# Edge lists laid out as 384 consecutive edges a partition, and tile 0 prepared ahead of a branch, in a graph attention and mixture-of-experts kernel

## The reference, cut to what matters

```python
def _gat_layer(x, W, a_src, a_dst, b, src, dst, n_nodes):
    h = x @ W
    e = leaky_relu((h @ a_src)[src] + (h @ a_dst)[dst], 0.2)
    m = segment_max(e, dst); w = exp(e - m[dst]); z = segment_sum(w, dst)
    return segment_sum(h[src] * (w / z[dst])[:, None], dst) + b
```

## Time and profile before

| what | us |
|---|---|
| median of 3 runs | 1493.97 (1488.02 to 1497.21) |
| the profiled execution | 1489.21 |
| its span | 1487.5 |
| PE busy | 1375.7 (92%) |
| DVE busy | 1126.6 (76%) |
| ACT busy | 914.1 (61%) |
| POOL busy | 436.6 (29%) |
| granted clock, mean | 0.975 |

### The profile page before, as it was taken

One profiled execution on the slowest core, in us unless ns is written; L12 is line 12 of the kernel. 1 busy time (PEld: TensorE's weight loads), 2 busy tenths in 40 slices (PEclk: granted clock), 3 DMA queues, 4 the chain that ended last, 5 costly groups with the idle time before them and its releaser, 6 DMA issues.

```text
span 1487.5 us, 25322 instructions
## 1 busy us (share of the span) xinstructions
PE 1375.7 (92%) x8889; PEld 1319.7 (89%) x8889; DVE 1126.6 (76%) x1543; ACT 914.1 (61%) x1601; POOL 436.6 (29%) x335
## 2 busy tenths in 40 slices
PE   2996999899799999899999999999998997799997
PEld 2995988899699999799999999999997997699997
DVE  5888998635889653586868868778688887788885
ACT  6887777322467322447847568486687421699995
POOL 1000000000000010335636446265476400355553
PEclk9997999999899999999999999999999998799999
DMA  7001000221334620000000000000011596376651
GB/s 202 8 1 42 16 25 23 71 92 38 105 94 145 195 86 0 22 1 2 21 1 21 0 0 21 0 21 0 0 32 40 154 294 146 118 169 166 162 103 26
DMA packets 48640, 99.17 MB, mean 67 GB/s; under 512 B 7178, under 2 KB 23182, under 8 KB 48554
## 3 DMA queue, kind: packets, MB, share of 16 engines
q1 hardware_dynamic: 40787, 75.04, 16.2%
q0 software_dynamic: 7488, 22.26, 7.5%
q10 hardware_dynamic: 279, 0.77, 0.2%
HBM read 67.23 MB, written 33.70 MB: 68 GB/s over the span
## 4 chain that ended last, share of the span: by engine, by line
PE 65%; DVE 6%; issue 3%; ACT 2%; DMA 2%; POOL 1%; ACTq 0%; POOLq 0%; SPq 0%; DVEq 0%
PE ps L421 13%; PE ps L422 13%; PE ps L423 13%; PE ps L912 5%; PE ps L957 4%; PE ps L959 4%; PE ps L958 3%; PE ps L936 3%; PE ps L938 3%; DVE mcol L1181 1%; POOL prlo L1144 1%; PE ps L1370 1%; PE ps L661 1%; DVE prlo L1144 1%; ACT prob L1082 1%
## 5 line engine op out<-in xcount | busy, mean ns | idle before, releaser
L1144 POOL TENSOR_TENSOR prlo<-prob,prhi 125x500 fp32r<-125x500 f32 x180 | 257.0, 1434 | 250.1 <-ACT prob L1082 249.2
L1181 DVE TENSOR_REDUCE mcol<-ps 125x1 f32<-125x1250 f32 x120 | 175.0, 1459 | 76.2 <-PE ps L912 74.1
L1080 ACT ACTIVATE prhi<-ps 125x500 fp32r<-125x500 f32 x300 | 176.8, 589 | 72.0 <-PE ps L938 65.3
L957 PE MATMUL ps<-prhi,vhi 125*128 125x250 f32 x600 | 171.6, 286 | 10.4 <-POOL prlo L1144 6.9
L1082 ACT ACTIVATE prob<-ps 125x500 f32<-125x500 f32 x300 | 176.1, 587 | 0.7 <-DVE prlo L1144 0.6
L959 PE MATMUL ps<-prlo,vhi 125*128 125x250 f32 x600 | 168.0, 280 | 0.0
L958 PE MATMUL ps<-prhi,vlo 125*64 125x250 f32 x600 | 167.0, 278 | 0.0
L936 PE MATMUL ps<-qst,kst 128*125 128x250 f32 x600 | 155.7, 283 | 2.7 <-ACT val L614 1.1
L421 PE MATMUL ps<-hhi,pthi 125*125 125x384 f32 x400 | 155.0, 388 | 3.0 <-DVE ptlo L784 3.0
L938 PE MATMUL ps<-q,k 128*125 128x250 f32 x600 | 153.4, 280 | 0.0
L1666 POOL MEMSET q<- 128x2500 f32 x1 | 2.2, 2185 | 503.3 <-PE ps L423 503.3
(11 more groups left out here) (343 smaller groups left out, 3849.7 us busy)
## 6 DMA issues: line engine op xcount, KB each, us to landing
w1all<-in_L_ffn_W_dram SPq DMA_DIRECT2D x8, 1152.0 KB, 9.0
w2st<-in_L_ffn_W_dram SPq DMA_DIRECT2D x8, 1152.0 KB
wqst<-in_L_ffn_Wqkv_dram SPq DMA_DIRECT2D x12, 384.0 KB, 4.2
hid_d<-tin SPq DMA_DIRECT2D x10, 375.0 KB
hin<-hid_d SPq DMA_DIRECT2D x10, 375.0 KB
vtin<-xn_d SPq DMA_DIRECT2D x10, 375.0 KB
out_dram<-accr POOLq DMA_DIRECT2D x10, 375.0 KB, 8.3
xres<-in_x_dram SPq DMA_DIRECT2D x10, 336.0 KB
```

The lines of the kernel that those rows point to most:

```text
L957: pe.matmul(ps[:, b:b + GQ], vhi[:, e, kt, :], hi, start=kt == 0, stop=False)
L1080: act.activation(prhi[:, n % RING, :], bank(3 + n % 3, P, 2 * GQ), ACT.Exp, scale=float(HD) ** -0.5)
L1144: eng.tensor_tensor(prlo[:, n % RING, :], prob[:, n % 3, :], prhi[:, n % RING, :].bitcast(f32), ALU.subtract)\
L1181: dve.tensor_reduce(mcol[:, e, t:t + 1], ps[0:P, 0:N], AX.X, ALU.max, negate=True).then_inc(sem("max"), 1)
```

## The change

1. **Edge layout.** One partition holds 384 consecutive edges: `sraw` is [128, 384], `draw` [128, 62 + 384]. Loads: destinations rows 1 to 95 (1784 bytes each), sources rows 0 to 95 (1536 bytes), the first destination row; then, after GpSimd (POOL) has set rows 96 to 127, rows 96 to 106 of both, and the last partial row of both: seven loads for eight. The transposes are still six of 128 x 128, now into banks 4 and 5, and the copy out of them writes with a stride of three columns.
2. **Copies over two engines.** ACT copies and divides the sources (`edges_src`), DVE copies the destinations alone.
3. **Tile 0 ahead of the branch.** Its moments go from ACT to DVE (MOMENTS_DVE starts at 0), its scale, normed copy, transposes, upper and lower half stand ahead of the branch, as does the first `ohs` batch. PE turns tile 0 before it waits for the flag.
4. **Order of ACT before the loop.** Only 8 edge values are made before it (20 before); in the loop two a step until it is 20 ahead (`digits_until`). All six `whi` and normed tile 1 stand before the loop.
5. **Products of tile 0.** `first1` takes all products with `whi` first (24, chunk by chunk), then the 12 with `wlo`.
6. **Places.** FIRST 8 to 0, with it all projections, the handover and the first turn eight steps earlier (TURN0 151 to 143); TURN 31 to 32; `destinations(b)` at least 5b + 1 for 4b - 3; WEIGHT1_AT, moments and scales moved as below.

```diff
-FIRST, PERIOD, PARTS = 8, 12, 13
-TURN0, TURN, EARLY, SLOTS = FIRST + 143, 31, 12, 21
+FIRST, PERIOD, PARTS = 0, 12, 13
+TURN0, TURN, EARLY, SLOTS = FIRST + 143, 32, 12, 21
-MOMENTS_DVE = tuple(range(2, T, 2))
+MOMENTS_DVE = tuple(range(0, T, 2))
-WEIGHT1_AT = (2, 3, 5, 6, 7, 9)
+WEIGHT1_AT = (5, 6, 9, 10, 11, 13)
+def digits_until(g):
+    return min(g + min(AHEAD, 8 + g), STEPS)
...
+            sp.dma_start(draw[1:96, :], dst_rows(1, 96)).then_inc(sem("edges_in"), 16)
+            sp.dma_start(sraw[0:96, :], src_rows(0, 96)).then_inc(sem("edges_in"), 16)
+            sp.dma_start(draw[0:1, MOST:], dst[0:384].rearrange("(p k) -> p k", p=1)).then_inc(sem("edges_in"), 16)
             sp.wait_ge(sem("set_pool"), ERAW_CLEAR)
+            sp.dma_start(draw[96:full, :], dst_rows(96, full)).then_inc(sem("edges_in"), 16)
+            sp.dma_start(sraw[96:full, :], src_rows(96, full)).then_inc(sem("edges_in"), 16)
+            sp.dma_start(draw[full:full + 1, 0:MOST + some], dst_rows(full, full + 1, MOST + some)).then_inc(sem("edges_in"), 16)
+            sp.dma_start(sraw[full:full + 1, 0:some], src[384 * full:EDGES].rearrange("(p k) -> p k", p=1)).then_inc(sem("edges_in"), 16)
...
+            def first1(i):
+                for n in range(3 * i, 3 * i + 3):
+                    if n < 4 * KD:
+                        k, h, x1 = n // 4, n // 2 % 2, (txhi, txlo)[n % 2]
+                        if n % 4 == 0:
+                            pe.wait_ge(sem("w_hi"), k + 1)
+                        pe.matmul(bank(4 + h, P, HALF), x1[:, 0, k * P:(k + 1) * P], whi[:, k, h * HALF:(h + 1) * HALF],
+                                  start=n < 4 and n % 2 == 0, stop=False)
+                    else:
+                        k, h = n // 2 - 2 * KD, n % 2
+                        if h == 0:
+                            pe.wait_ge(sem("w_lo"), k + 1)
+                        last = pe.matmul(bank(4 + h, P, HALF), txhi[:, 0, k * P:(k + 1) * P], wlo[:, k, h * HALF:(h + 1) * HALF],
+                                         start=False, stop=k == KD - 1)
...
-                        if t and g == linear(t - 1, 0):
+                        if t and g == linear(t - 1, 6 if t == 1 else 0):
                             transposes1(t)
...
+            moments1(1)
+            act.wait_ge(sem("start_pe"), EDGES_T)
+            act.activation(edge[:, 0, LEAD:].rearrange("q (p c) -> q c p", c=3), bank(4, 128, 384).rearrange("q (c p) -> q c p", c=3), ACT.Copy)\
+                .then_inc(sem("edges_src"), 1)
+            act.wait_ge(sem("edges_src"), 1)
+            act.activation(digit[:, 0, :], edge[:, 0, 0:NCOLS], ACT.Identity, scale=1.0 / DIGITS, bias=viol[:, 6:7])\
+                .then_inc(sem("edges_src"), 1)
+            root1(0)
+            rooted1(1)
+            normed(0)
+            weights1(0)
+            higher1(0)
             act.wait_ge(sem("start_dve"), VALUES)
             for g in range(4):
                 valued(g)
+            weights1(1)
+            weights1(2)
+            valued(4)
+            valued(5)
+            weights1(3)
+            valued(6)
+            valued(7)
+            weights1(4)
+            weights1(5)
+            normed(1)
...
-                if g + AHEAD < STEPS:
-                    valued(g + AHEAD)
+                for q in range(digits_until(g), digits_until(g + 1)):
+                    valued(q)
-                    if t >= 2 and g == max(linear(t - 3, 6), 4 * t + 3):
+                    if t >= 2 and g == max(linear(t - 3, 6), 4 * t):
-                    if t and g == linear(t - 1, 4):
+                    if t and g == linear(t - 1, 9 if t == 1 else 4):
                         higher1(t)
-                    if t and g == linear(t - 2, 9):
+                    if t >= 2 and g == max(linear(t - 2, 9), 10):
                         normed(t)
...
+            dve.wait_ge(sem("edges_in"), 112)
+            dve.tensor_copy(efl[:, 1, :, :], draw[:, MOST:].rearrange("p (c k) -> p c k", c=3))
+            dve.tensor_copy(efl[:, 0, :, :], sraw[:, :].rearrange("p (c k) -> p c k", c=3)).then_inc(sem("start_dve"), 1)
...
+            moments1(0)
+            dve.wait_ge(sem("start_pe"), EDGES_T)
+            order.did(dve.tensor_copy(edge[:, 1, LEAD:].rearrange("q (p c) -> q c p", c=3),
+                                      bank(5, 128, 384).rearrange("q (c p) -> q c p", c=3)))
...
+            rstd1(0)
+            dve.wait_ge(sem("rows_paired"), 2)
+            destinations(0)
+            dve.wait_ge(sem("edges_src"), 2)
...
+            step_near(0)
+            lower1(0)
+            spread = dve.value_load(flag[0:1, 0:1], min_val=0, max_val=1)
```

More of the change, by code:

```diff
@@ L183, in build @@
     mcol = put("mcol", [P, 2, T], f32)
-    viol = put("viol", [128, 6], f32)
+    viol = put("viol", [128, 8], f32)
     FREE = top[0]
@@ L243, in build @@
     assert put.end <= FREE + 2 * 4 * KD * N + 32
-    sraw = put("sraw", [128, 3, 128], i32, at=FREE)
-    draw = put("draw", [128, 3, MOST + 128], i32, at=put.end)
+    sraw = put("sraw", [128, 384], i32, at=FREE)
+    draw = put("draw", [128, MOST + 384], i32, at=put.end)
     efl = put("efl", [128, 2, 3, 128], f32, at=put.end)
@@ L1425, in _ @@
         def _(sp):
[L1427 to L1434, removed]
@@ L1764, in _ @@
                 for c in range(3):
-                    last = pe.transpose(ps[:, a * BANK + c * 128:a * BANK + (c + 1) * 128], efl[:, a, c, :], ident[:, :])
+                    last = pe.transpose(ps[:, (4 + a) * BANK + c * 128:(4 + a) * BANK + (c + 1) * 128], efl[:, a, c, :], ident[:, :])
             last.then_inc(sem("start_pe"), 1)
[L1767 to L1772, removed]
             def transposes1(t):
@@ L1787, in triple1 @@
                 if t == 0:
-                    pe.wait_ge(sem("w_lo"), k + 1)
+                    first1(i)
+                    return
                 last = three(pe, bank(4 + 2 * u + h, P, HALF), txhi[:, u, k * P:(k + 1) * P], txlo[:, u, k * P:(k + 1) * P],
@@ L1859, in first_layer @@
                                 triple_sum(pe, 0, t, t % 2, i)
+            transposes1(0)
+            pe.wait_ge(sem("start_dve"), VIOL)
+            for c in (0, 4, 5):
+                last = pe.matmul(ps[0:1, 2 * BANK:2 * BANK + 1], viol[:, c:c + 1], viol[:, 1:2], start=c == 0, stop=c == 5)
+            last.then_inc(sem("start_pe"), 1)
+            pe.wait_ge(sem("start_dve"), FLAG)
+            spread = pe.value_load(flag[0:1, 0:1], min_val=0, max_val=1)
             pe.wait_ge(sem("set_pool"), TABLES)
@@ L2151, in _ @@
             order.did(dve.memset(viol[:, 2:3], FAR))
+            order.did(dve.memset(viol[:, 6:7], 0.5 / DIGITS - 0.5))
             dve.wait_ge(sem("set_pool"), ERAW_CLEAR)
[L2153 to L2161 removed]
             def relative(j):
@@ L2382, in first_layer @@
                         lower2(dve, 0)
-                    if near and g < STEPS:
+                    if near and 0 < g < STEPS:
                         step_near(g)
+            s_, d_ = edge[:, 0, 0:NCOLS], edge[:, 1, :]
+            quarter, node, value = (digit[:, i, :] for i in range(3))
+            real = slice(LEAD, LEAD + EROWS)
+            dve.wait_ge(sem("edges_in"), 112)
+            dve.tensor_copy(efl[:, 1, :, :], draw[:, MOST:].rearrange("p (c k) -> p c k", c=3))
+            dve.tensor_copy(efl[:, 0, :, :], sraw[:, :].rearrange("p (c k) -> p c k", c=3)).then_inc(sem("start_dve"), 1)
@@ new lines, in _ @@
+            order.wait()
+            order.did(dve.scalar_tensor_tensor(lohi[:, 0, real], d_[:, real], 0.0, lohi[:, 0, real], ALU.add, ALU.is_lt,
+                                               accum_out=viol[:, 0:1]))
+            order.did(dve.scalar_tensor_tensor(lohi[:, 1, real], d_[:, real], 0.0, lohi[:, 1, real], ALU.add, ALU.is_ge,
+                                               accum_out=viol[:, 4:5]))
+            relative(0)
+            order.wait()
+            dve.sem_inc(sem("start_dve"), 1)
@@ new lines, in _ @@
+            rstd1(0)
+            dve.wait_ge(sem("rows_paired"), 2)
+            destinations(0)
+            dve.wait_ge(sem("edges_src"), 2)
+            order.did(dve.tensor_scalar(node, quarter, ROUNDER, -ROUNDER, ALU.add, ALU.add))
+            order.wait()
+            order.did(dve.scalar_tensor_tensor(value, node, -float(DIGITS), s_, ALU.mult, ALU.add))
+            order.did(dve.tensor_copy(scol[:, :], node))
+            order.wait()
+            dve.wait_ge(sem("start_pe"), VIOL_SUM)
@@ new lines, in _ @@
+            dve.tensor_scalar(flag[0:1, 0:1], ps[0:1, 2 * BANK:2 * BANK + 1], 0.0, None, ALU.is_gt).then_inc(sem("start_dve"), 1)
+            dve.wait_ge(sem("start_dve"), FLAG)
+            dve.tensor_scalar(sval[:, :], value, float(6 << 23), float(127 << 23), ALU.mult, ALU.add).then_inc(sem("start_dve"), 1)
+            order.did(dve.tensor_copy(scodd[:, :], scol[:, ODD:ODD + ODDS]))
+            dve.wait_ge(sem("set_pool"), TABLES)
+            order.wait()
+            step_near(0)
```

(1 more changed line is left out.)

91 lines of the change are left out of this document (25 added, 66 removed).

## The result

| what | before | after |
|---|---|---|
| median us (lowest to highest) | 1492.57 (1488.02 to 1497.21), 20 runs | 1494.05 (1492.32 to 1500.38), 20 runs |
| ratio after / before | | 1.0021 (1.0012 to 1.003) |
| the profiled execution | 1489.21 | 1496.99 |
| its span | 1487.5 | 1495.2 |
| granted clock, mean | 0.975 | 0.969 |

The changed kernel is slower by 0.21% (0.12% to 0.30%), 3.1 us; this ratio is taken over all runs, the two medians alone stand 1.5 us apart. The three runs that I had of before gave a median of 1493.97, twenty give 1492.57, so the forecast's starting point was 1.4 us high as well. The loss is within 1% and inside the range, but on the other side of zero from the 5.5 us faster that I forecast. The profiled executions stand 7.7 us apart, more than the medians, so they are read for places and mechanisms, and the runs for the size.

What follows compares the result with a forecast made beforehand. TensorE's idle time before 44 us, behind late edges, was taken as the prize. 7.5 us gained ahead of tile 2, less 1.5 handed back and 0.5 in the handover, gave 5.5 faster: 1488.5 us, eight-in-ten range 1481.5 to 1496.

Steps and rivals of the forecast that it cites:

- after 271.5 us nothing is edited: Scope of the forecast: the change touches the schedule only up to there, so the prize is TensorE's idle time before 44 us.
- the one rival that ended slower (handover, 0.06): Handover to the attention sums: VectorE's run pushed 2.5 us, deferred steps cost 3, 5.5 go back; 1496.5 us, chance 0.06.
- The landing: Start of the kernel: edges seen at 7.3 us instead of 12.7, with transfers at 351 GB/s.
- The condition that I named for being wrong: Start: x lands later because the weights press in 3 us earlier, moving the anchor A one for one.
- The upper bound in the text, near 10.5: Landing: one engine still carries the 95-row load's 169 KB at 25 GB/s, 6.8 us alone.
- only a small gain: Rival: landing stays near 10 to 12 or VectorE remains late; gain 0 to 2.5 us, 1492.5, chance 0.2.
- From landing to tile 2: Front: tile 2 starts at anchor A + 37.3; with A = 7.7 at 45.0, 7.5 us earlier than before.
- The branch: After tile 0's lower half: crossing costs 0.9 us of VectorE that nothing of its own covers, ending at A + 10.1.
- Cold start: Rival: TensorE enters tile 1 at the low clock, costing 1.6 us more; gain 3.9, 1490 us, chance 0.12.
- The new wait: After the branch: VectorE waits 3.2 us from A + 17.8 for ScalarE's root of tile 2, and 1.9 for root(3).
- Handed back: After the handover: eight deferred count steps cost 1.5 us (0.5 to 3); the handover itself adds 0.5 (-1 to 2.5).
- more than 8 us: Rival: batches of steps 16 and 24 don't stall TensorE, eight steps find idle slots in the turns; 1484, chance 0.15.

Runs made afterwards that it cites:

- e5: The changed kernel with three no-op semaphore increments more in ScalarE's stream before the second layer: 1487.67 us, ratio 0.9973 to the kernel before.
- e7: The changed kernel with 50 no-op semaphore increments more in ScalarE's stream before the second layer: 1487.35 us, ratio 0.9977 to the kernel before.
- e4: The changed kernel with one no-op more on ScalarE and the load of 95 destination rows split into 80 and 15: 1495.31 us, ratio 1.002.
- e1: The changed kernel with one no-op semaphore increment more in ScalarE's stream before the second layer: 1496.07 us, ratio 1.0031 to the kernel before.
- e6: The changed kernel with 103 no-op semaphore increments more in ScalarE's stream before the second layer: 1490.55 us, ratio 1.0003 to the kernel before.
- e9: The changed kernel with three no-ops on ScalarE and projection put back eight steps (FIRST 8, TURN 31): 1489.63 us, ratio 0.9994.
- e2: The kernel before with one redundant ScalarE wait (root of tile 8) left out: 1500.81 us, ratio 1.0054.
- e8: The changed kernel with three no-ops on ScalarE, tile 2's root sooner and the 95-row load split: 1483.78 us, ratio 0.9951.
- e3: The changed kernel with one no-op more on ScalarE, tile 2's root at step 3 and the last weight half at 11: 1495.80 us, ratio 1.0024.
- e10: The changed kernel with three no-ops, early root, split load, and window 2's unpacking and destinations 12 sooner: 1485.33 us, ratio 0.9965.

## Why the prediction was wrong, step by step

**The sign, the step that failed:** "after 271.5 us nothing is edited", and so nothing was summed there. The sum held only work, waits and transfers; it had no term for where the unchanged loop comes to lie in ScalarE's instruction stream. e5 and e7 against after put that term at 0.46 points of ratio, 6.9 us. No rival named it, and the one rival that ended slower (handover, 0.06) had the right sign for the wrong reason: at 300 us after was 3.6 us ahead, so the handover hadn't eaten the gain. Its 1496.5 doesn't follow from its own prices either: 5.5 us given back against the 5.0 that the front gained would be 0.5 slower.

**The landing, the term that was mis-sized:** 7.3 us forecast, 10.26 measured. I had taken a bandwidth of 351 GB/s until the last byte. The condition that I named for being wrong held: the weights are issued at 3.52 instead of behind 7.1 us, and the DMA engines, 0.08 busy from 7 to 8 us in the earlier trace rows, are full. The stretch of after:

```profile
7.00:8.00 1.00, 0.00 (x0) 0.00 (x0) 0.00 (x0) 0.00 (x0) 0.71 (x4) 1.00 1.09 272
```

x comes at 9.23, 0.8 later than before. By e4 the one load of 95 rows costs 1.4 of it. The upper bound in the text, near 10.5, came out nearly right by luck: it had one engine carry the 95 rows alone, at 25 GB/s, while here all engines are busy at 272. What the rival "only a small gain" said of the landing, that it stays near 10 to 12, is what happened. The Trainium skill, "DMA: Bandwidth & Descriptors", section on why a DMA increments its semaphore by 16, gives five engines for 95 rows; no view here shows how many it ran on. The landing near 7 that I drew from it left out with what else the engines are shared.

**From landing to tile 2:** the sum came out, in part by luck. The formula A + 37.3 with A = 10.26 gives 47.56; measured 47.53. Its parts: normed tile 0 at A + 4.8 = 15.1 (14.93), transposes' end at A + 7.4 = 17.7 (17.5), first product at A + 9.2 = 19.5 (20.30: VectorE stood 0.95 us for TensorE's sum before it could make the flag, at 17.86, and the one-hots and the lower half slid behind it). The branch, on the other hand, showed no pause of 0.9 us on VectorE. Two larger errors behind it cancel as well; they stand under "Cold start". In e1, e5, e6 and e7 the same way takes 36.5 to 37.7 us.

**The new wait:** right in place and cause, 3.94 us for 3.2, at 31.5 us; corrected for the landing, the forecast's end is at 31.3. Root(3): 2.27 for 1.9.

**Handed back:** forecast 1.5 + 0.5 = 2.0. Measured from tile 2 to the second layer 1.4 in after, 1.2 to 2.7 with e1, e5, e6 and e7: right as a sum; how it splits between deferred steps and handover isn't separated. e9 shows that the deferral wins more ahead of tile 2 (2.3 to 3.5) than this.

**Cold start:** the clock did fall. Behind the wait of 1.58 us the first products of tile 1 take half again as long as later ones, 0.53 us for 0.34:

```profile
37.75 0.53 PE L426 MATMUL ps<-whi,txlo 128*125 128x384 f32 x1
...
38.07 0.53 PE L427 MATMUL ps<-wlo,txhi 128*125 128x384 f32 x1
```

The busy time of that stretch has the granted clock at half, too:

```profile
34.20:41.00 6.80, 5.22 (x20) 4.67 (x19) 4.35 (x10) 5.75 (x15) 0.00 (x0) 0.50 0.20 71
```

Yet tile 2 started when the formula said, because a wait that I had summed didn't come: 0.9 and 0.8 us for the one-hot batches of steps 16 and 24. TensorE has no wait between 36.10 and 47.53, as the rival "more than 8 us" had it for these batches. From tile 1's first product to tile 2's it takes 10.5 us; in before, at full clock and also without a wait, 8.6. So the low clock cost up to 1.9 us, near the rival's 1.6, and took the place of 1.7 us of waits.

**The sum redone** with the measured landing: 5.0 ahead of tile 2, less 2.0, is 3.0 us faster. e5 and e7, the change without the placement, are 4.0 and 3.4 faster. Less 6.9 for the placement, 3.0 becomes 3.9 slower; measured 3.1 (1.8 to 4.5).

**What stays open.** The steps of the shift outside 795 to 1110 us (about +2.5 before it and +2.2 behind it in after) come in some executions and not in others. The one near 1160, about 1 us, goes with the clock: the mean granted clock from 1155 to 1190 us is 0.95 in e2, e4, e6 and e8, and in after and e5 it stands at 0.50 for 3.4 us from 1170.8 and 1163.1; these six have the step. In before, e1, e3, e7, e9 and e10 the clock there is 1.00 and there is no step, though the wait ahead of it, about 1.57 us for a lower half, is the same in before, after, e5 and e9. What makes the clock fall in one execution and not in another wasn't tested. Nor is it shown why four blocks don't stay resident.

## What to carry to other kernels

Before pricing an edit in one part of an unrolled program, look at the loops behind it: count the instructions that each engine has ahead of a loop, and compare the instruction queue's packets inside the loop, before and after; if they appear, no-ops ahead of the loop can give the time back (here 3 or 50 did, 1 and 103 did not). When transfers are moved earlier, list what is issued behind them, because that is now what they share the DMA engines with. A wait for one engine's result is only removed when the next result in the same order comes earlier as well.

## What the runs showed of the hardware

- A ScalarE loop of 287 instructions runs without fetching at start places 961 and 1008 and fetches five packets of 8192 bytes on each of its passes after the first at 958, 959, 960 and 1061. Each jump back then leaves ScalarE idle for 2.3 (e6) to 3.9 us (e2), 3.1 at the first of after, and the kernel pays 3.4 to 14 us in three jumps. The second of the two pauses behind a jump comes where place 961 is reached, after 3, 2 or 1 rows of the loop.
- The same stall costs different amounts: 1.6 us at the first jump of after with the granted clock at 1.00, 3.1 at the third, where it fell to 0.50 for some 3 us behind waits of 1.23 and 0.98 us.
- An activation with an accumulated sum takes two places in ScalarE's instruction stream. By the instructions of the program alone the loop starts at 949 both in before, which doesn't refetch, and in e1, which does; with the accumulating ones (12 and 10) counted twice they are 961 and 959.
- A load of 95 rows, split as 80 and 15, brought itself and the x rows on another queue 1.4 us earlier each (e1 to e4: casts 9.83 to 8.39, x 9.13 to 7.69).
